# A gated four-layer block with experts: the sorted row tiles of layer 3 stay in SBUF and are turned once each

## The reference

```
w, sel = _routing(x, gate_w)                     # top 4 of 32, weights sum to 1
cw_large = zeros((T, 32)).at[rows, sel].add(w)
cw_small = zeros((T, 16)).at[rows, sel // 2].add(w)
large = _moe(x, Wg, Wu, Wd, cw_large)            # silu(x Wg) * (x Wu) * cw, times Wd; inner size 96
small = _moe(x, cWg, cWu, cWd, cw_small)         # the same for pairs of experts; inner size 128
out = x_in + tanh(g_ffn[3]) * (large + 0.05 * small)
```

## Time and profile before

| what | value |
|---|---|
| median of three runs | 1278.52 us (1273.51 to 1278.64) |
| the profiled execution: its time, its span | 1275.05 us, 1273.3 us |
| mean granted TensorE clock | 0.914 of full speed |
| busy: PE, DVE, ACT, POOL | 84%, 65%, 53%, 53% of the span |
| 63 expert steps | 1073.43 to about 1254 us |
| from the last scatter's start to the end | 16.3 us |

### The profile page before, as it was taken

One profiled execution on the slowest core, in us unless ns is written; L12 is line 12 of the kernel. 1 busy time (PEld: TensorE's weight loads), 2 busy tenths in 40 slices (PEclk: granted clock), 3 DMA queues, 4 the chain that ended last, 5 costly groups with the idle time before them and its releaser, 6 DMA issues.

```text
span 1273.3 us, 18231 instructions
## 1 busy us (share of the span) xinstructions
PE 1068.6 (84%) x5382; PEld 834.3 (66%) x5382; DVE 822.8 (65%) x1515; ACT 677.3 (53%) x1718; POOL 675.0 (53%) x452
## 2 busy tenths in 40 slices
PE   6576788778747978999999999798999746999993
PEld 3455577656514766888888888665555444888883
DVE  3892799689779751666666565859998683333332
ACT  4466555444554235778787777467663124333331
POOL 2105888888823232444454545429997103786653
PEclk8888799899958998999999999989999857999997
DMA  6494999897440013011101110305542993877655
GB/s 189 140 199 120 238 287 292 214 278 175 55 131 1 1 51 92 16 59 51 54 18 55 54 50 2 104 1 154 153 141 55 268 270 101 182 166 130 104 73 132
DMA packets 153171, 154.49 MB, mean 121 GB/s; under 512 B 35188, under 2 KB 140396, under 8 KB 153076
## 3 DMA queue, kind: packets, MB, share of 16 engines
q1 hardware_dynamic: 129092, 123.04, 33.5%
q0 software_dynamic: 22896, 29.24, 14.2%
q10 hardware_dynamic: 1088, 1.05, 0.2%
HBM read 123.11 MB, written 30.18 MB: 120 GB/s over the span
## 4 chain that ended last, share of the span: by engine, by line
PE 54%; POOL 16%; DVE 12%; issue 8%; DMA 5%; ACT 3%; SPq 0%; POOLq 0%; DVEq 0%; ACTq 0%
PE bank L2496 8%; POOL f_sums L1023 6%; PE bank L1600 4%; PE bank L1696 4%; PE bank L1685 4%; PE bank L1663 4%; POOL arena L1009 4%; PE bank L1589 2%; DMA f_sums<-arena,put 2%; PE bank L1618 2%; PE bank L1674 2%; PE bank L2125 2%; PE bank L2514 2%; PE bank L2516 2%; POOL arena L560 2%
## 5 line engine op out<-in xcount | busy, mean ns | idle before, releaser
L540 DVE TENSOR_TENSOR_SCAN arena<-arena 128x1024 f32<-128x1024 f32 x64 | 155.3, 2427 | 19.7 <-issue 12.2
L1023 POOL DMA_INDIRECT f_sums<-arena,put x64 | 124.0, 1937 | 22.8 <-issue 17.7
L560 POOL TENSOR_TENSOR arena<-arena 128x1024 f32<-128x1024 f32 x32 | 82.4, 2574 | 88.8 <-DVE arena L540 88.8
L2393 POOL DMA_INDIRECT e_sums<-ctxT,put x63 | 98.7, 1567 | 57.0 <-DVE ctxT L2695 40.1
L1009 POOL DMA_INDIRECT arena<-y_rows,slots x64 | 82.8, 1294 | 67.2 <-DVEq L1224 45.9
L2496 PE MATMUL bank<-arena,ssm_y 128*128 x504 | 108.4, 359 | 0.4 <-issue 0.4
L518 ACT ACTIVATE arena<-arena,ssm_A 128x255 f32<-128x255 f32 x256 | 108.0, 498 | 0.2
L2125 PE MATMUL bank<-yT,arena 128*128 128x512 f32 (+1 forms) x224 | 103.2, 605 | 3.3 <-ACT arena L2056 3.3
L570 PE MATMUL bank<-arena,ident 128*128 128x256 f32 x256 | 72.2, 431 | 33.9 <-DVE arena L560 30.5
L2689 DVE TENSOR_TENSOR ssm_y<-ssm_y,bank 128x256 f32<-128x256 f32 x63 | 26.6, 422 | 114.2 <-ACT ssm_y L2571 68.1
L529 DVE TENSOR_TENSOR arena<-arena 128x1024 f32<-128x1024 f32 x64 | 94.3, 1473 | 0.0
(11 more groups left out here) (343 smaller groups left out, 2722.8 us busy)
## 6 DMA issues: line engine op xcount, KB each, us to landing
arena<-bc_rows SPq DMA_DIRECT2D x64, 512.0 KB
y<-e_sorted SPq DMA_DIRECT2D x62, 128.0 KB
arena<-in_L_ffn_w_gate_dram SPq DMA_DIRECT2D x16, 256.0 KB
arena<-in_L_ffn_w_up_dram SPq DMA_DIRECT2D x16, 256.0 KB
arena<-in_L_ffn_w_down_dram SPq DMA_DIRECT2D x16, 256.0 KB
x<-in_L_ffn_w_gate_dram SPq DMA_DIRECT2D x16, 256.0 KB
y<-in_L_ffn_w_up_dram SPq DMA_DIRECT2D x16, 256.0 KB
yT<-in_L_ffn_w_down_dram SPq DMA_DIRECT2D x16, 256.0 KB
```

The source lines that it names most:

```text
L540: nc.vector.tensor_tensor_scan(ssm_h[:, j % 2, :], ssm_decay[:, j % 2, :], ssm_in, 0.0, ALU.mult, ALU.add).then_inc(s_ssm_h, 1)
L560: ops.tensor_tensor(ssm_hC_buf[:, j % 2, :], ssm_h[:, j % 2, :], ssm_C[:, g % 2, :], ALU.mult).then_inc(s_ssm_hC, 1)
L1023: nc.gpsimd.indirect_dma_start(out=f0_sums[m % SUMS], out_offset=bass.IndirectOffsetOnAxis(ap=put[:, m:m + 1], axis=0), in_=f0_ye[:, n % R ...
L2393: nc.gpsimd.indirect_dma_start(out=e_sums[t % 2], out_offset=bass.IndirectOffsetOnAxis(ap=put[:, t:t + 1], axis=0), in_=e_ye[:, t % 4, :], ...
```

## The change

- x, y, yT and ctxT become parts of one array `rows32` of 32 tiles: y is tiles 0 to 7, yT 8 to 15, ctxT 16 to 19, x 24 to 31. Two weight arrays of layers 1 and 3 (`win_rows`, `winT`) move into tiles 20 to 23. The ring `e_ye` moves from ctxT into other memory.
- POOL gathers sorted tile t into `rows32[:, t]`, where it stays. There is no `e_sorted`: SP's 32 stores, its 62 register reads and its 62 loads are gone.
- `e_first[u]` is the earliest step in which tile u can be needed: 0 to 8 for tiles 0 to 8, then 10 to 17, 19 to 26, 28 to 34. TensorE turns tile u once, in step e_first[u] - 2 (tiles 0 and 1 ahead of the loop). ACT copies it from PSUM back over the gathered rows (`tile_copy`).
- For each step ACT reads `e_tile[t]` into a register and copies that tile within SBUF from `rows32` into the ring `e_xgT`.
- POOL's gather of tile t stands ahead of scatter(e_first[t] - 8); tiles 0 to 8 go ahead of scatter(0).

```diff
+        rows32 = sb("rows32", [P, 32, D])
...
+        y = rows32[:, 0:NT, :]
+        yT = flat_rows(NT, NT).rearrange("p (h n) -> p h n", h=HD)
+        ctxT = flat_rows(2 * NT, T // D)
+        x = rows32[:, 32 - NT:32, :]
...
+        LEAD = 8
+        e_first = [t + max(0, t - 1) // (T // P) for t in range(FULL)]
...
-        e_ye = ctxT[:, :].rearrange("p (r n) -> p r n", r=4)
+        e_ye = scan_y[:, 0:4 * D].rearrange("p (r n) -> p r n", r=4)
...
-            keep(0)
-            keep(1)
-            wait(sp, s_e_tab, 2)
-            wait(sp, s_e_kept[0], 16)
-            for t in range(1, RUN):
-                if t + 1 < FULL:
-                    keep(t + 1)
-                if t < FULL:
-                    wait(sp, s_e_kept[t % 4], 16 * (t // 4 + 1))
-                if t >= XR:
-                    wait(sp, s_e_T, t - XR + 1)
-                of = sp.value_load(e_tile[0:1, t:t + 1], min_val=0, max_val=FULL - 1)
-                sp.dma_start(e_xg[:, t % XR, :], rows[ds(of, 1), :, :].rearrange("a p d -> p (a d)")).then_inc(s_e_xg[t % XR][0], 16)
...
+            def gather(t):
+                if t >= RING:
+                    wait(pool, s_e_sort[t % RING], 16 * (t // RING))
+                if t == FULL - NT:
+                    wait(pool, s_e_init, 16)
+                nc.gpsimd.indirect_dma_start(
+                    out=rows32[:, t, :], out_offset=None, in_=y_rows,
+                    in_offset=bass.IndirectOffsetOnAxis(ap=slots[:, t:t + 1], axis=0),
+                    oob_is_err=True).then_inc(s_e_sort[t % RING][0], 16)
+
+            for s in range(RUN):
+                for t in range(FULL):
+                    if e_first[t] == s + LEAD or (s == 0 and e_first[t] < LEAD):
+                        gather(t)
+                if s == 0:
+                    wait(pool, s_e_slots, 2)
+                scatter(s)
...
+            def turn(u):
+                wait(pe, s_e_sort[u % RING], 16 * (u // RING + 1))
+                if u >= 2:
+                    wait(pe, s_e_res, u - 1)
                 for h in range(HD):
-                    last = nc.tensor.transpose(bank[t_bank(r)][:, h * P:(h + 1) * P], rows[:, h * P:(h + 1) * P], ident[:, :])
+                    last = nc.tensor.transpose(bank[u % 2][:, h * P:(h + 1) * P], rows32[:, u, h * P:(h + 1) * P], ident[:, :])
                 last.then_inc(s_e_T[0], 1)
...
-                if not (static(t) and t + 1 >= RUN):
-                    turn(t + 1, (k + 1) % XR, turns + (k + 1) // XR)
+                for u in range(FULL):
+                    if e_first[u] == t + 2:
+                        turn(u)
...
+            def tile_copy(u):
+                wait(act, s_e_T, u + 1)
+                nc.scalar.copy(rows32[:, u, :], bank[u % 2][:, 0:2 * P]).then_inc(s_e_res[0], 1)
+
             def xgT_copy(t, r):
-                wait(act, s_e_T, t + 1)
-                if not (static(t) and t < 4):
+                wait(act, s_e_res, sum(first <= t for first in e_first))
+                if t >= 4:
                     wait(act, s_e_gu, t - 3)
-                nc.scalar.copy(e_xgT[:, r, :], bank[r % 2][:, 0:2 * P]).then_inc(s_e_xgT[0], 1)
+                of = act.value_load(e_tile[0:1, t:t + 1], min_val=0, max_val=FULL - 1)
+                nc.scalar.copy(e_xgT[:, r, :], rows32[:, ds(of, 1), :].rearrange("p a d -> p (a d)")).then_inc(s_e_xgT[0], 1)
```

More of the change, by code:

```diff
@@ L2325, in flamingo_kernel @@
         s_e_ld = (s_x_w[0], 16 * H // 2)
-        s_e_kept = [(s, 16 * SUMS) for s in s_f0_more]
-        s_e_more = [(s, 16 * SUMS + 16 * FULL // 4) for s in s_f0_more]
+        s_e_more = [(s, 16 * SUMS) for s in s_f0_more]
         s_e_x = (s_f0_x, B)
@@ L2395, in scatter @@
                     in_=e_ye[:, t % 4, :], in_offset=None, oob_is_err=True, compute_op=ALU.add).then_inc(s_e_st[t % 4][0], 16)
-            LATE = XR + 3
-            for t in range(RUN + LATE):
-                if t < FULL:
-                    if t >= RING:
-                        wait(pool, s_e_sort[t % RING], 16 * (t // RING))
-                    if t >= XR:
-                        wait(pool, s_e_kept[t % 4], 16 * ((t - XR) // 4 + 1))
-                    if t == XR:
-                        wait(pool, s_e_T, 1)
-                    nc.gpsimd.indirect_dma_start(
-                        out=e_new[:, t % XR, :], out_offset=None, in_=y_rows,
-                        in_offset=bass.IndirectOffsetOnAxis(ap=slots[:, t:t + 1], axis=0),
-                        oob_is_err=True).then_inc(s_e_sort[t % RING][0], 16)
-                if t >= LATE:
-                    scatter(t - LATE)
+            def gather(t):
[14 more added lines that the diff above has]
+                scatter(s)
         def e_route_pe(pe):
@@ L2459, in e_pe @@
             e_route_pe(pe)
-            def turn(t, r, turns):
-                if t:
-                    wait(pe, s_e_xg[r], (turns + (r > 0)) * 16)
-                    rows = e_xg[:, r, :]
-                else:
-                    wait(pe, s_e_sort[0], 16)
-                    rows = e_new[:, 0, :]
-                if not (static(t) and t < 2):
-                    wait(pe, s_e_xgT, t - 1)
+            def turn(u):
+                wait(pe, s_e_sort[u % RING], 16 * (u // RING + 1))
+                if u >= 2:
+                    wait(pe, s_e_res, u - 1)
                 for h in range(HD):
-                    last = nc.tensor.transpose(bank[t_bank(r)][:, h * P:(h + 1) * P], rows[:, h * P:(h + 1) * P], ident[:, :])
+                    last = nc.tensor.transpose(bank[u % 2][:, h * P:(h + 1) * P], rows32[:, u, h * P:(h + 1) * P], ident[:, :])
                 last.then_inc(s_e_T[0], 1)
-            def t_bank(r):
-                return r % 2
             read = {}
@@ L2523, in e_pe @@
             pe.wait_ge(s_e_pad, 1)
-            turn(0, 0, 0)
+            turn(0)
+            turn(1)
             wait(pe, s_e_slots, 2)
@@ L2577, in hT_copy @@
                 nc.scalar.copy(e_hT[:, r % 2, :], bank[4 + r % 2][:, 0:2 * P]).then_inc(s_e_hTc[0], 1)
+            tile_copy(0)
+            tile_copy(1)
+            wait(act, s_e_tab, 2)
             xgT_copy(0, 0)
             def step(t, k, turns):
+                for u in range(FULL):
+                    if e_first[u] == t + 2:
+                        tile_copy(u)
                 if not (static(t) and t + 1 >= RUN):
```

19 lines of the change are left out of this document (5 added, 14 removed).

## The result

The changed kernel takes 1267.01 us (median of 8 runs, 1260.51 to 1272.11), the kernel before 1277.15 us (8 runs); the ratio is 0.9919, 95% interval 0.9896 to 0.9943. It is faster by 0.8%, about 10 us. Its profiled execution took 1264.27 us with a span of 1261.6 us, 11.7 us less than before.

What follows compares the result with a forecast made beforehand. TensorE was taken to bound the steps, and tile 1's round trip the start. -6.8 (turns) - 4.6 (start) + 1.4 (late gathers) = -10.0 us, from 1276.4 to 1266.4, stated as 1267; range 1258 to 1275.

Steps and rivals of the forecast that it cites:

- Turns: TensorE's steps: each of 32 tiles turned once instead of 63 turns, 31 fewer at 0.22 us, -6.8 us.
- Start: Ahead of the first step: no round trip of tile 1, gate_up(0) at 1068.8 instead of 1073.43, -4.6 us.
- Clock: TensorE's half clock at the start: whole ramp moves with the start, half speed for as long as before, no gain.
- ACT: ACT in the steps: 32 more tile copies and register-addressed copies stay hidden behind TensorE, cost 0.
- its rival: ACT becomes the bound through exposed register reads ahead of xgT_copy: 1281 at 1.5 us, about 1312 at 2.0; chance 0.08.
- Gathers: POOL falls behind at 3.19 us a gather-scatter pair, so tile 31 is late at step 32: +1.4 us.
- The stalls are the same one, growing: Steps 30 to 32: tiles 29, 30, 31 late by 0.7, 1.0, 1.4 us, summing to only 1.4.
- idle in turns from step 20 on: Sign that the prediction is wrong through gathers: TensorE idle in turns from step 20; stalls expected only in 30 to 32.
- its rival of late gathers: Landing 6 us or pair 3.4: tile 31 late 4 to 6 us, gain only 5 to 7, 1271; chance 0.15.
- SP's traffic at 0: SP's removed stores and loads: no TensorE time hung on them except in the start, so 0.
- Tail: End of the stage: late scatters catch up long before step 62, cost 0; at 2.49 us each, 1.8 us left.
- The register load: ACT's register work per step: 1.04 us, measured on SP, taken over the skill's 1.3, which would lose 3.3 us.

Runs made afterwards that it cites:

- extra_turns: Changed kernel with a turn of the identity matrix put back on TensorE alone in steps 33 to 62; stage 190.73 us, time 1273.65 us, ratio to before 0.9979.
- act_reads4: Changed kernel with four register reads of e_tile ahead of each xgT_copy on ACT instead of one; stage 195.58 us, time 1283.88 us (1 run).
- sp_traffic: Changed kernel with SP's traffic put back as 31 stores and 62 copies of 128 KB that nobody needs; stage 186.09 us, time 1269.08 us (1 run).
- LEAD 12: Changed kernel with each tile's gather issued 12 scatters ahead instead of 8; stage 182.02 us, time 1264.93 us, ratio to before 0.9894.
- lead12_regs: Changed kernel with gathers 12 scatters ahead instead of 8 and TensorE's e_tab register read ahead of the turn; stage 181.99 us, time 1269.11 us, ratio 0.9915.
- lead10_start: Changed kernel with gathers 10 scatters ahead, turn(2) behind gate_up(0), xgT_copy(0) ahead of tile_copy(1), tile_copy(2) behind silu(0); stage 183.67 us, time 1269.62 us.
- LEAD 10: Changed kernel with gathers 10 scatters ahead instead of 8; alone, stage 183.73 us, time 1269.58 us, ratio to before 0.9923; lead10_start also has it.

## Why the prediction was right

Forecast -10.0 us and 1267; measured -10.1 us by the medians, with -10.34 in the stage. The mechanism was right in both places, the turns and the start, and each gain has a run of its own. That the median is 1267.01 is luck: the interval of the ratio reaches from -7.3 to -13.3 us, and within the stage the terms were off by up to 1 us in both directions. By the stretches they are -7.04 for the 32 turns that left the steps (turn(2) now stands ahead of gate_up(0)), -4.84, -0.85, +2.45 and -0.06, which make the -10.34.

- **Turns.** -6.8 forecast for 31. By extra_turns 0.21 to 0.22 each, 6.5 to 6.8; right.
- **Start.** -4.6 forecast, -4.84 measured, and every time of it within 0.25 us: turn(1) 4.3 us behind gather 0 (4.4 forecast), xgT_copy(0) 5.9 (6.0), gate_up(0) 6.46 (6.7). ACT's register chain was shorter than the 1.04 us of the earlier trace rows: xgT_copy(0) starts 0.91 us behind tile_copy(1), in the steps about 0.68 where nothing else holds it.
- **Clock.** Forecast that the ramp moves along whole, at nothing; it gave 0.85 us. The half clock ended 6.0 us behind turn(1) instead of 6.6, and gate_up(0) stood 2.20 us behind turn(1) instead of 1.04. So from gate_up(0) on 3.8 us ran at half clock instead of 5.6, and half of that difference is 0.9. The prediction's own times (gate_up(0) 2.3 us behind turn(1), the clock back at 6.6) would have given 0.6; it put the term at nothing without reckoning it.
- **ACT.** Right at 0. The price of its rival was too high. By its formula the 1.88 us that stand bare in act_reads4 cost 30 x 0.69 + 33 x 0.54 = 38.5 us; the steps lost 10.5 us in the two stretches above. The formula adds up whole durations, but ACT starts one instruction before the last one's row ends: in that run silu starts 0.31 us behind a copy of 0.40, and hT_copy 0.28 behind a silu of 0.38.
- **Gathers.** The mechanism was right, the term of +1.4 mis-sized: 2.45 us. Step 32 was reckoned as 29 steps of 2.82, though steps 7, 16 and 25 have no turn: 0.66 us earlier. From gather 31 to gate_up(32) it took 3.76 us, where landing and turn were reckoned as 3.4 + 0.22 = 3.62: 0.14 more. Two errors hide in this 0.14: the landing took 2.8 and not 3.4, and behind it stood 0.96 us with the register work and not 0.22. That makes 1.4 + 0.66 + 0.14 = 2.2, and gate_up(32) was 2.17 late. The other 0.28 came in the three steps behind it (2.75, 2.70 and 2.63 us for 2.60), for a reason that no run shows. "The stalls are the same one, growing" held; but they began at step 24, and 1.9 of the 2.45 us came from step 29 on. So the sign against the prediction, idle in turns from step 20 on, nearly came true: it is the effect of its rival of late gathers at about half the price, though neither cause of that rival (a landing of 6 us, a pair of 3.4) was there.
- **SP's traffic at 0.** Not quite: by sp_traffic 1.4 us would be lost with it in the middle. The prediction put the landing at 3.4 us, as read with SP's stores and loads; without them its median is 2.8, and with the copies of sp_traffic 3.8. The Trainium skill (DMA: Bandwidth & Descriptors, "Queues, rings and completion order") has each DMA engine take turns between the queues that have work, from which I had worked out 3.0; these numbers agree with that rule, and 3.0 would have been the better choice.
- **Tail.** Right: scatters were on time again at scatter(41), and scatter(62) comes 7.98 us behind the last gate_up against 8.04.
- **The register load.** The 1.3 us of the Trainium skill (Runtime: NRT & Kernel Launch, "The ~15µs preamble/postamble breakdown") are for loads from HBM at a launch and no guide to a read from SBUF: 0.54 us per read on ACT, measured by act_reads4.

## What to carry to other kernels

Where an engine is busy without a gap, an instruction taken off it is worth the difference between a step with it and one without (0.22 us for a turn, whose row shows 0.38), and a stage's first instruction is worth a chain of waits read event by event; the sum of both stood within 0.5 us, with the 0.85 us of the clock apart. A prefetch that is issued behind another queue's late work drifts with that work: its lead must be counted in the queue's own pace (3.20 us a pair here against steps of 2.82), with the steps that are shorter than usual taken in, and up to the instruction that the wait really holds up, not only the first one behind it. A few steps more of lead cost nothing here (LEAD 12, -2.5 us in the stage). And a read of a register placed behind an instruction that may wait is hidden only as long as it doesn't wait.

## What the runs showed of the hardware

- The whole program's time varies by 9 to 14 us between executions of one kernel (1275.48 to 1284.87 us for 14 of the kernel before, 1260.51 to 1272.11 for the changed kernel, 1260.09 to 1274.18 for lead12_regs). Most of it arises ahead of this stage: gather 0 starts between 1060.14 and 1069.51 us in the profiles of programs that are the same up to there, while what follows the stage varies by 1.7 us. Two kernels that should not differ in the stage, lead12 and lead12_regs, took 182.02 and 181.99 us in it. Changes of 2 or 3 us are settled by stretches of the trace, not by medians.
- TensorE's clock was granted for some 4 us more behind the routing's last matmuls (which end at about 1059.6 us), was 0.50 (1.2 GHz) from 1064, and was at 0.90 in 1070 to 1072 (changed kernel, PE alone: busy, clock, DMA share, GB/s):

```profile
1062.00:1064.00 2.00, 0.41 (x2) 0.90 0.39 115
1064.00:1066.00 2.00, 1.07 (x4) 0.50 0.37 98
...
1070.00:1072.00 2.00, 2.00 (x12) 0.90 0.33 82
```

  It came back 5.7 to 6.0 us behind turn(1) in the ten profiles in which gate_up(0) came 1.2 to 2.4 us behind turn(1); so what lead10_start won at gate_up(0) ran at half clock. In act_reads4, where gate_up(0) came 3.8 us behind turn(1), it came back only 9.4 us behind it.
- An instruction on ACT, silu(1), stood still for over 2 us with no releaser in the trace, in both kernels with LEAD 10 and in none of the twelve others. Its cause is open.
